# A state-space block with a mixture of experts: decays in SBUF, paired scans, smaller expert tiles

## The reference

```
s:  u = xn + mamba(rmsnorm(xn));  s = u + silu(rmsnorm(u) @ W1.T) @ W2.T
    mamba: xp, z = split(x @ in_proj.T)            # 512 channels each
           xc = silu(causal_conv4(xp))             # 4 taps along time
           dt, B, C = from xc @ x_proj.T           # dt: softplus, 512 channels; B, C: 16 states
           h[d, n] = exp(dt[d] * A[d, n]) * h[d, n] + dt[d] * xc[d] * B[n]    # along time
           y[d] = sum_n h[d, n] * C[n] + D[d] * xc[d]
           out = (y * silu(z)) @ out_proj.T
g:  gate = softmax(xn @ gate_w + gate_b)           # 8 experts
    top two experts per token: g = silu(sum gate_e * (relu(xn @ w1_e + b1_e) @ w2_e + b2_e))
out = x + s * g
```

## Time and profile before

| | |
|---|---|
| runs, median (lowest, highest) | 1691.06 us (1690.83, 1693.83) |
| profiled execution, its own time | 1688.73 us |
| its span, first to last instruction | 1686.9 us |
| granted TensorE clock, mean | 0.904 of full speed |
| busy: TensorE / VectorE / GpSimd / ScalarE | 1376.1 / 1270.1 / 1191.7 / 909.1 us |
| chain that ended last, shares | TensorE 48%, VectorE 13%, GpSimd 11%, ScalarE 9%, issue 9% |
| largest group: scans, line 1238 | 512 x 1285 ns = 657.8 us |
| GpSimd: `dbu`, line 644; sums of `hxc`, line 660 | 602.5 us; 386.6 us |

### The profile page before, as it was taken

The page is one execution under the profiler, slowest core; times in us unless marked ns, Lnnn a source line. Parts: engine busy times, 40 slices in busy tenths (PEclk is TensorE's granted clock), DMA queues, the critical chain, the costliest instruction groups (busy, mean ns, idle before and its releaser), DMA issues.

```text
span 1686.9 us, 17807 instructions
## 1 busy us (share of the span) xinstructions
PE 1376.1 (82%) x5328; PEld 1000.2 (59%) x5328; DVE 1270.1 (75%) x1545; ACT 909.1 (54%) x1967; POOL 1191.7 (71%) x619
## 2 busy tenths in 40 slices
PE   3565272988989898989899898899997989778677
PEld 1442022766677666766687666676776668645355
DVE  7469762887977897879778987889788968768522
ACT  3532333565575656665757565755756465535441
POOL 3523885775798679767797779767986798787830
PEclk9577775999999899989999999999999999879789
DMA  8713443754377436753486437544764447455530
GB/s 315 288 44 112 165 144 142 244 179 154 125 248 241 150 119 202 258 178 125 159 283 200 158 127 262 182 167 133 244 245 148 170 162 273 153 162 178 174 110 25
DMA packets 124321, 301.46 MB, mean 179 GB/s; under 512 B 14376, under 2 KB 26800, under 8 KB 113984
## 3 DMA queue, kind: packets, MB, share of 16 engines
q1 hardware_dynamic: 109200, 262.28, 45.8%
q0 software_dynamic: 9024, 27.27, 4.7%
q10 hardware_dynamic: 6000, 10.75, 1.9%
HBM read 258.57 MB, written 41.68 MB: 178 GB/s over the span
## 4 chain that ended last, share of the span: by engine, by line
PE 48%; DVE 13%; POOL 11%; ACT 9%; issue 9%; DMA 1%; DVEq 0%; SPq 0%; ACTq 0%; POOLq 0%
PE prod L909 38%; DVE state L1238 7%; PE ysum L961 5%; POOL dbu L644 4%; POOL slot_x L631 3%; POOL hxc L660 2%; ACT state L719 2%; DVE prod L1263 1%; DVE hxc L1249 1%; PE prod L914 1%; POOL late L691 1%; PE prod L1082 1%; ACT late L880 1%; PE prod L949 1%; DVE late L1309 1%
## 5 line engine op out<-in xcount | busy, mean ns | idle before, releaser
L1238 DVE TENSOR_TENSOR_SCAN state<-state,carry,dbu 128x512 f32<-128x512 f32 x512 | 657.8, 1285 | 218.6 <-ACT state L719 171.4
L644 POOL TENSOR_TENSOR dbu<-dtu,bb 128x1024 f32<-128x1024 f32 x256 | 602.5, 2360 | 81.5 <-DVE state L1238 76.4
L660 POOL TENSOR_TENSOR hxc<-hxc 128x1024 f32<-128x1024 f32 x164 | 386.6, 2357 | 246.9 <-DVE hxc L1249 246.8
L719 ACT ACTIVATE state<-dt,par 128x512 f32<-128x512 f32 x512 | 353.5, 692 | 106.2 <-DVE hxc L1249 91.0
L1249 DVE TENSOR_TENSOR hxc<-state,cb 128x512 f32<-128x512 f32 x512 | 354.3, 692 | 44.7 <-DVE state L1238 2.4
L909 PE MATMUL prod<-late 128*128 128x256 f32 x1248 | 302.6, 401 | 42.2 <-issue 15.6
L909 PEld LDWEIGHTS prod<-late 128*128 128x128 f32 x1248 | 256.5, 208 | 86.0 <-issue 46.3
L909 PE MATMUL prod<-xsT,late 128*128 128x256 f32 x1248 | 292.0, 386 | 9.7 <-DVE xc L1273 5.9
L909 PEld LDWEIGHTS prod<-xsT,late 128*128 128x128 f32 x1248 | 239.9, 194 | 65.9 <-issue 21.9
L961 PE MATMUL ysum<-hxc,ident 128*128 128x512 f32 x368 | 200.4, 673 | 84.0 <-POOL hxc L660 30.4
L717 ACT COPY carry<-state 128x1 f32<-128x1 f32 x384 | 61.3, 160 | 235.6 <-DVE hxc L1249 228.6
(11 more groups left out here) (152 smaller groups left out, 1263.2 us busy)
## 6 DMA issues: line engine op xcount, KB each, us to landing
bb<-bc_rows SPq DMA_DIRECT2D x256, 256.0 KB, 5.6
cb<-bc_rows SPq DMA_DIRECT2D x256, 256.0 KB, 4.1
late<-moe SPq DMA_DIRECT2D x39, 1028.0 KB, 4.9
late<-moe SPq DMA_DIRECT2D x39, 1024.0 KB, 5.3
slot_x<-xc POOLq DMA_DIRECT2D x20, 512.0 KB, 11.7
xs<-slot_x SPq DMA_DIRECT2D x39, 256.0 KB, 5.7
slot_y<-ys ACTq DMA_DIRECT2D x39, 256.0 KB, 3.5
late<-x SPq DMA_DIRECT2D x12, 512.0 KB, 8.6
```

Source lines behind the costliest of these rows:

```text
L644: nc.gpsimd.tensor_tensor(dbu[:, v % 3, :, :], dtu[:, n % 2, 2 * h:2 * h + 2, :], b, ALU.mult).then_inc(dbu_ready, 1)
L660: nc.gpsimd.tensor_tensor(hxc[:, to, :, :], hxc[:, to, :, :], hxc[:, piece, :, :], ALU.add).then_inc(summed, 1)
L719: nc.scalar.activation(state[:, k % 2, :], dt[:, n % 2, 2 * h + k % 2, :], ACT.Exp, scale=par[:, P_ALOG + col(k):P_ALOG + col(k) + 1]).the ...
L1238: nc.vector.tensor_tensor_scan(state[:, c, :], state[:, c, :], dbu[:, v % 3, c, :], carry[:, n % 2, col(k):col(k) + 1], ALU.mult, ALU.add) ...
```

## The change

It has several parts:
- **Decays.** ScalarE writes them into `decays`, four buffers in SBUF, three steps ahead (`AHEAD`). The scan reads `decays` and `dbu`, both in SBUF, and writes `state` in PSUM.
- **Pairs.** VectorE does scan, scan, product with C, copy of both last columns into `carry`, product with C. ScalarE no longer copies into `carry`.
- **Groups.** The last block has 11 GpSimd sums instead of 20; TensorE adds more groups there.
- **Experts.** 31 tiles of 256 slots and 9 of 128, interleaved (`M_ORDER`), over steps 62 to 474. A half tile has 16 UP products of 128 columns instead of 256, and 8 DN products instead of 16; it loads the full weights.
- **Router.** Transposes and logits stand in the prologue (`FIRST`), before the first decay in ScalarE's order. The layernorm of the blocks behind the first (28 token tiles) moves from VectorE to GpSimd. Ranking takes two maxima instead of comparing all pairs; RO pieces stand at steps 2 to 10. The scatter is spread over steps 11 to 57.
- **Combination.** The last three blocks are mixed by VectorE (AD: four multiply-adds into PSUM for each half) and not by diagonal products; the gathers of the first five stand apart in the order.
- Smaller buffers make room: `dt` has three halves, `xpad` two chunks with a `halo` for each; DTA1 and DTU1 stand at steps 64 and 68, part of the MLP a few steps later.

```diff
-TILES = (2 * BATCH * SEQ + NE * (SLOTS - 1)) // SLOTS
-ZTILES = TILES + 1
+UNITS = 2 * BATCH * SEQ // P + NE - 1
+PAIRS = (UNITS - NE) // 2
+TILES = UNITS - PAIRS
+Z_ROWS = (UNITS + 3) // 4 * 4 * P
...
-GROUPS = [((1,) * NS,) * 2] + [((4,) * 4,) * 2] * (NB - 2) + [((4,) * 4, (2,) * 8)]
+GROUPS = [((1,) * NS,) * 2] + [((4,) * 4,) * 2] * (NB - 2) + [((4,) * 3 + (1,) * 4, (2,) * 2 + (1,) * 12)]
 HX = 5
+AHEAD = 3
...
+FIRST = """A.LOADX A.XR A.TR0 A.TR1 R.TX00 R.TX01 L.L1 L.L2 L.L3 A.IN0 A.IN1 L.L4 L.L5 L.L6 L.L7 L.ROOT L.XN
+ A.CV0 A.TH0 A.IN2 A.CV1 A.TH1 A.IN3 A.SL0 R.LG0 A.CV2 A.TH2 A.SL1 R.TX10 A.CV3 A.TH3 A.SL2 R.TX11 A.SL3 A.HKEEP
+ R.LG1 A.XD0 A.XD1 A.BOUT R.TX20 R.TX21 R.LG2 A.DT0 A.DT1 A.DT2 A.DT3 R.TX30 R.TX31 R.LG3 A.SPE A.SPL R.TX40 R.TX41 R.LG4 R.TX50 R.TX51
+ A.DTA0 A.DTU0 A.DTA1 A.DTU1 R.LG5 R.TX60 R.TX61 R.LG6 R.TX70 R.TX71 R.LG7"""
+R_AT = 2
+M_ORDER = sorted(range(TILES), key=lambda i: (i + 0.5) / PAIRS if i < PAIRS else (i - PAIRS + 0.5) / (TILES - PAIRS))
...
+M_FROM, M_TO = 62, NK - 38
+D_VECTOR = 5
+D_STEPS = [{"GA": M_TO + 1 + 7 * g, "MX": M_TO + 11 + 7 * g} for g in range(5)] + [
+    {"GA": NK + 2, "MX": NK + 16}, {"GA": NK + 10, "MX": NK + 36}, {"GA": NK + 16, "MX": NK + 54, "FI": NK + 59}]
...
-        out[R_AT + 9 + t].append(("R", "SC%d" % t, None))
+        out[R_AT + 9 + t * 3 // 2].append(("R", "SC%d" % t, None))
...
+        for i in range(2 * NT):
+            out[at["GA"] + (i * 7 // 8 if g < 5 else 0)].append(("D", "G%d" % i, g))
...
+    work = [(w, t) for t in range(TILES) for w in m_work(t)]
...
+        decays = sb("decays", [P, AHEAD + 1, BT])
...
+                elif kind == "L" and name == "XN":
+                    pool.wait_ge(ln_root, 2)
+                    for t in range(NT, AT):
+                        nc.gpsimd.tensor_scalar(xn_all[:, t, :], xn_all[:, t, :], mv[:, t, 0:1], roots[:, 0, t:t + 1],
+                                                ALU.subtract, ALU.mult).then_inc(xn_ready, 1)
...
-                if k >= 2:
-                    act.wait_ge(hc_ready, k - 1)
-                if 2 <= k < (NB - 2) * BASE_STEP + 2:
-                    b = (k - 2) // BASE_STEP % 2
-                    nc.scalar.copy(carry[:, b, col(k - 2):col(k - 2) + 1], state[:, k % 2, BT - 1:BT]).then_inc(carried, 1)
-                    act.wait_ge(carried, k - 1)
-                nc.scalar.activation(state[:, k % 2, :], dt[:, n % 2, 2 * h + k % 2, :], ACT.Exp,
+                if k > AHEAD:
+                    act.wait_ge(scanned, k - AHEAD)
+                nc.scalar.activation(decays[:, k % (AHEAD + 1), :], dt[:, (2 * n + h) % 3, k % 2, :], ACT.Exp,
                                      scale=par[:, P_ALOG + col(k):P_ALOG + col(k) + 1]).then_inc(decay_ready, 1)
...
-                    decay(0)
+                    for k in range(AHEAD):
+                        decay(k)
                 elif kind == "S":
-                    if i + 1 < NK:
-                        decay(i + 1)
+                    if i + AHEAD < NK:
+                        decay(i + AHEAD)
...
-                        for r in range(2):
-                            hc = 2 * pair + r
-                            last = products(dst[:, r * SLOTS:(r + 1) * SLOTS], lambda k: w1v[:, k, hc * P:hc * P + P],
-                                            lambda k: xsT[:, k, :], KC)
+                        for j in range(BT // cols):
+                            hc = int(name[2]) * (BT // cols) + j
+                            last = products(dst[:, j * cols:(j + 1) * cols], lambda k: w1v[:, k, hc * P:hc * P + P],
...
-                        for k in range(2):
-                            pe.matmul(dst, diag[b][:, k, t, :], gy[b][:, k, t, :], start=(k == 0), stop=False)
-                        last = pe.matmul(dst, gate_t[:, t * P:t * P + P], b2, start=False, stop=True)
+                        if by_diag:
+                            for k in range(2):
+                                pe.matmul(dst, diag[b][:, k, t, :], gy[b][:, k, t, :], start=(k == 0), stop=False)
+                        last = pe.matmul(dst, gate_t[:, t * P:t * P + P], b2, start=not by_diag, stop=True)
                     last.then_inc(*is_full(key))
...
-                    k, v = i, i // 2
+                    if i % 2:
+                        return
+                    v = i // 2
                     n, h, s = unit(v)
-                    c = k % 2
-                    if s == 0 and c == 0 and h == 0 and n >= 2:
-                        dve.wait_ge(carried, (n - 1) * BASE_STEP)
-                    dve.wait_ge(decay_ready, k + 1)
-                    dve.wait_ge(dbu_ready, v + 1)
-                    nc.vector.tensor_tensor_scan(state[:, c, :], state[:, c, :], dbu[:, v % 3, c, :],
-                                                 carry[:, n % 2, col(k):col(k) + 1], ALU.mult, ALU.add
-                                                 ).then_inc(scanned, 1)
+                    if s == 0 and h == 0 and n >= 2:
+                        dve.wait_ge(carried, (n - 1) * 2 * NS)
+                    for c in range(2):
+                        k = i + c
+                        dve.wait_ge(decay_ready, k + 1)
+                        if c == 0:
+                            dve.wait_ge(dbu_ready, v + 1)
+                        if v:
+                            dve.wait_ge(hc_ready, k - 1)
+                            if c == 0:
+                                dve.wait_ge(carried, v)
+                        nc.vector.tensor_tensor_scan(state[:, c, :], decays[:, k % (AHEAD + 1), :], dbu[:, v % 3, c, :],
+                                                     carry[:, n % 2, col(k):col(k) + 1], ALU.mult, ALU.add
+                                                     ).then_inc(scanned, 1)
                     buf, what = HX_OF[v]
-                    if c == 0:
-                        dve.wait_ge(cb_in[v % 4], 16 * (v // 4) + 16)
-                        if what and what[0] == "summed":
-                            dve.wait_ge(summed, what[1])
-                        elif what:
-                            dve.wait_ge(y_acc, what[1])
-                    dve.wait_ge(scanned, k + 1)
-                    nc.vector.tensor_tensor(hxc[:, buf, c, :], state[:, c, :], cb[:, v % 4, :],
-                                            ALU.mult).then_inc(hc_ready, 1)
+                    dve.wait_ge(cb_in[v % 4], 16 * (v // 4) + 16)
+                    if what and what[0] == "summed":
+                        dve.wait_ge(summed, what[1])
+                    elif what:
+                        dve.wait_ge(y_acc, what[1])
+                    for c in range(2):
+                        dve.wait_ge(scanned, i + c + 1)
+                        nc.vector.tensor_tensor(hxc[:, buf, c, :], state[:, c, :], cb[:, v % 4, :],
+                                                ALU.mult).then_inc(hc_ready, 1)
+                        if c == 0:
+                            dve.wait_ge(scanned, i + 2)
+                            nc.vector.tensor_copy(carry[:, n % 2, col(i):col(i) + 2],
+                                                  state[:, :, BT - 1:BT].rearrange("p c t -> p (c t)")).then_inc(carried, 1)
...
+                elif kind == "D" and name[:2] == "AD":
+                    b, q = i % 2, int(name[2])
+                    key = (kind, "MX%d" % q, i)
+                    at = 8 * (i - D_VECTOR) + 4 * q
+                    full(dve, key)
+                    if q == 0:
+                        dve.wait_ge(gathered[b], 16 * 2 * NT * (i // 2 + 1))
+                    for k in range(2):
+                        for r in range(2):
+                            t = 2 * q + r
+                            dst = bank(key)[:, r * DM:r * DM + DM]
+                            if k:
+                                dve.wait_ge(d_add, at + r + 1)
+                            nc.vector.scalar_tensor_tensor(out=dst, in0=gy[b][:, k, t, :],
+                                                           scalar=gates[:, k, i * NT + t:i * NT + t + 1], in1=dst,
+                                                           op0=ALU.mult, op1=ALU.add).then_inc(d_add, 1)
```

More of the change, by code:

```diff
@@ L159, in events @@
         out[fi + 1].append(("D", "ST", g))
-    work = [(w, t) for t in range(TILES) for w in M_WORK]
+    work = [(w, t) for t in range(TILES) for w in m_work(t)]
     other = [sum(cost(kind, name) for kind, name, i in slot) for slot in out]
@@ L180, in steps @@
     later = LATER.get(engine, {})
-    return [(k, e) for k, q, e in sorted((k + later.get(kind, 0), q, (kind, name, i))
+    return [(k, e) for k, q, e in sorted((k + later.get(name[:2] if kind == "C" else kind, later.get(kind, 0)), q, (kind, name, i))
                                          for q, (k, kind, name, i) in enumerate(EVENTS))]
@@ L477, in walk @@
                 do(kind, name, i)
-                for norm in L_AFTER.get(name, ()):
-                    do("L", norm, None)
             do("S", "FIRST", None)
@@ L875, in do @@
```

(34 more changed lines are left out.)

268 lines of the change are left out of this document (137 added, 131 removed), and 8 rows, old and new, of tables (STEPS_A, STEPS_C).

## The result

The changed kernel takes 1935.02 us (median of 4 runs, 1930.21 to 1940.04) against 1690.94 (4 runs, 1687.63 to 1693.83): a ratio of 1.1444, 95% interval 1.1401 to 1.1488. Its profiled execution has a span of 1937.4 us at a mean granted TensorE clock of 0.85.

A forecast was written before the change was run, and what follows sets the result against it. The prediction took scans and GpSimd instructions, excluding each other at SBUF, to bound the changed kernel: 260 + 19 - 14 - 14 = +251 on 1688.7 us gives 1940. The range to hold 8 times in 10 was 1715 to 2050.

The forecast's parts named there:

- until step 64: Start and block 0: ends near 301 us instead of 314.8, -14; bounds +7, -25 and +59.
- first scan: Start: five router groups stay exposed, +27 us, so the first scan moves from 60.8 to 88.
- six full blocks: Blocks of 64 steps: scans and GpSimd products never run together, 223.7 us a block, +260; bounds +206 and +376.
- last block: Last block: fewer sums, but uneven work and gathers; 207 us against 188, +19, between 0 and +50.
- tail: Behind the last scan: twelve groups of diagonal products dropped, 13.6 us of TensorE; -14, between 0 and -20.
- sum: Whole kernel: 260 + 19 - 14 - 14 = +251, on 1688.7 us, so 1940.
- What the scan reads: Scans: with two SBUF inputs, scan and GpSimd product exclude each other both ways; scan mean above 1.8 us; chance 0.68.
- pull opposite ways: Six blocks: handover gaps and the shortening of waiting operations offset each other, so 6.99 us a pair was taken.
- What hid: Six blocks: TensorE's 54 us of tile work, decay waits (171.4) and ScalarE's carry copies (61.3) save nothing beside the port.
- bounded this at +59: Block 0, 46 scatter steps: if indirect issues exclude scans, 46 x 1.285 = +59 us.
- Only VectorE waits: Rival, six blocks: GpSimd isn't held up by scans; +79 there, about 1740 us whole, 1690 to 1800; chance 0.17.
- The scans don't meet the port: Rival: no contention, so decay waits go and TensorE's saved 54 us counts; about 1611 us whole; chance 0.10.

The follow-up runs named there:

- e7: e1 with only the two decay buffers moved from PSUM to SBUF: 1949.61 us, ratio 1.1575 to the kernel before.
- e1: Changed kernel with decays back in PSUM, one step ahead, single steps and carry copies on ScalarE: 1606.88 us, ratio 0.9531 to the kernel before.
- e5: Changed kernel whose scan reads its own state in PSUM instead of dbu, so one SBUF input; computes another result: 1539.81 us, ratio 0.9134.
- e8: e1 with the decays of even steps in SBUF, those of odd steps in PSUM: 1797.65 us, ratio 1.0671 to the kernel before.
- e4: Changed kernel with GpSimd's sums two steps later in its order: 1862.02 us, ratio 1.1036 to the kernel before.
- e6: e1 with all eight combinations mixed by TensorE's diagonal products, none by VectorE: 1622.19 us, ratio 0.9622 to the kernel before.

## Why the prediction was right

Each term, measured from the two profiled executions (the boundary of the last block is now read at step 448, 1397.8 us before):

| term | forecast | measured |
|---|---|---|
| until step 64 | -14 | 301.9 - 314.8 = -12.9 |
| first scan | at 88 | at 87.2 |
| six full blocks | +260 | 1334.9 - 1083.0 = +251.9 |
| last block | +19 | 207.4 - 187.7 = +19.7 |
| tail | -14 | 93.2 - 101.4 = -8.2 |
| sum | +251 | +250.5 |

**What the scan reads.** Right, and shown: e7 changes one operand's place against e1, e5 one operand against the changed kernel, e8 that of every second scan, and the durations follow the number of SBUF inputs each time. The prediction took the waits to go both ways, and they do: the scans wait for the ends of products, and GpSimd's products take 2.35 or 3.3 us. The rule of the Trainium skill (SBUF — State Buffer, "Who interferes with whom") is that this lock is exclusive and lasts for the whole instruction. The trace agrees: the products at 906.91 and 252.77, one issued at the start of a scan and one near its end, end 2.16 and 2.17 us behind it.

**The six blocks.** The size was right, 222.5 us a block for 223.7, but by a sum that isn't the law behind it, and that it came out so close is luck. Two errors stand against each other. The sum takes full durations, but a waiting instruction needs some 0.2 us less behind its release, on both sides (the prediction allowed 0.14 for scans alone, in a bound): a scan or a GpSimd product or sum runs for 204.2 us a block, not 223.7. And "VectorE's two products with `cb` and the carry copy lie under GpSimd's share" holds only in part: GpSimd's sum waits for the second of these products, 2.4 us in the timeline above, so the port idles for 18.3 us a block, in part behind this wait. The remark that gaps and shortening "pull opposite ways" named both and sized neither. What sets the block, as I read it, is VectorE's own order of work with GpSimd instructions let in before and between the two scans of a pair: VectorE has no more than 26.4 of 1334.9 us idle. In the mean, its scans take 926.7 us where e5's take 471.4: 455 us over 192 pairs, 2.4 us a pair, just about one product.

**What hid.** The gains in TensorE's tiles, the decays ahead and the carry were given no effect beside the port. For decays ahead, pairs and carry that is nearly so: they are worth 15 us there (e7 to the changed kernel) and 67 with a free port (e1 to e5). For the tiles no run shows it; in e1 the other parts together are worth 78 us. VectorE's wait for decays is 2.6 us, "near none" as forecast. TensorE is busy for 1048 of 1334.9 us, 79% and not near 70, or 175 us a block for 155, at a mean clock of 0.88 instead of 0.96. The carry copies cost VectorE 141 ns each, 36.1 us in all.

**The start.** The first scan and step 64 came out, with one price wrong: GpSimd's norm takes 1213 ns a tile, 33.8 us, not 9 to 17. It ends at 60.8 us and stayed hidden, because the router's groups run to 85. Step 11 was at 128.5 instead of 138, and the 46 steps from there took 149.5 us (until 278.0), not 139: the scatter's indirect issues wait as well, 1258 ns in the mean against 982. I had bounded this at +59 and taken nothing. So step 64 came out near 301 because these two errors of 10 us cancel.

**The tail.** It is 8 us shorter, and not 14. In e1, with the same tail, it is 79 us at a clock of 0.89, and here 93 at 0.79. The four diagonal products of a group behind the last scan take 2.08 us here (at 1851.00) and 1.13 in e1 (at 1526.62), so TensorE is at the lower of its two levels there:

```profile
1851.00 2.08 PE L1117 MATMUL prod<-late,xs 128*128 128x256 f32 x4
```
```profile
1526.62 1.13 PE L1120 MATMUL prod<-late,xs 128*128 128x256 f32 x4
```

The conflict alone doesn't do it: in e7 and e4, whose scans meet GpSimd as well, the tail is 80 and 82 us at clocks of 0.89 and 0.90. What lowers the clock here stays open. e6 gives the VectorE mixing its 15 us.

**The rivals.** "Only VectorE waits" falls with the products of 3.3 us. "The scans don't meet the port" was priced at 1611 us; e1, where they don't, takes 1607, though e5, with the changed kernel's own order, goes to 1540, so I probably priced it too dear.

## What to carry to other kernels

Count the SBUF inputs of each long VectorE instruction before moving a buffer out of PSUM: with two of them and GpSimd busy with products, each such instruction can cost a GpSimd instruction's length, and now and then two. A few small operations in the trace of the kernel before, longer than their twins and ending where GpSimd ends, were enough to see it. And when a forecast made from a sum of occupations comes out, half the dose tells whether the sum was the mechanism.

## What the runs showed of the hardware that was not expected

- The waits go both ways and last until the other's instruction ends. Behind its release a waiting scan needs 1.09 us (1.28 alone) and a waiting product 2.16 (2.35 alone). A product that is issued near the start of a scan is 0.94 us late, one issued 0.94 us into it 0.16.
- GpSimd's indirect DMA issues are held up too: in the changed kernel one takes 1.75 us at 159.94 us, behind a scan, and the next 0.97. In e1, with no scan at the port, their mean is 987 ns.
- GpSimd's `tensor_scalar` over 128 x 256 takes 1.21 us, where a product over 128 x 1024 takes 2.36.
- Between two VectorE scans issued one behind the other, GpSimd's waiting instruction is let in, as at 906.36. The other way round it is mostly so, but at 293.99 a scan waits for two GpSimd products in a row.
